# One decoder layer in float32: the output projection as three fp32r passes with weights streamed from DRAM, cross products and a bias at other steps, zeroing at other steps

## What is computed

```
x = x + attn(layernorm(x))      # 16 heads of 128, rope, causal softmax, out = sum_heads z @ W_O + b_O
x = x + xattn(layernorm(x))     # kv products of 8 x 8 channels, causal convolution with k, skip, product with ctx
x = x + moe(layernorm(x))       # 16 experts, top 4, and a shared expert
```

## Time and profile before

| | |
|---|---|
| median of 3 runs | 970.07 us (969.96 to 970.83) |
| the profiled execution | 968.15 us |
| its span, first to last instruction | 966.3 us |
| PE / DVE busy | 97% / 79% |
| ACT / POOL busy | 41% / 42% |
| mean granted clock of PE | 0.988 of full |
| moved by DMA | 161.22 MB, 167 GB/s mean |

### The profile page before, as it was taken

How to read it: one execution, slowest core, us unless ns; L and a number is a source line. 1 busy time by engine, 2 the same in 40 slices (tenths; PEclk the granted TensorE clock), 3 DMA queues, 4 the chain that set the end, 5 groups by cost and what they waited for, 6 DMA issues and landing times.

```text
span 966.3 us, 18710 instructions
## 1 busy us (share of the span) xinstructions
PE 935.6 (97%) x6081; PEld 830.0 (86%) x6081; DVE 761.1 (79%) x1692; ACT 392.9 (41%) x1153; POOL 407.4 (42%) x320
## 2 busy tenths in 40 slices
PE   6999999999999999999999999988999999999997
PEld 6788888988888888898888888876887799999985
DVE  6878967877877888777788976677677988888867
ACT  3546444443323444233364332352245444444430
POOL 1312313154412125465213546404725267777760
PEclk9999999999999999999999999999999999999998
DMA  7963297421078932205967450225151277878769
GB/s 272 314 238 144 104 353 281 185 89 65 1 247 301 373 132 89 77 35 184 329 229 281 156 178 23 98 91 213 57 208 65 60 124 131 130 129 133 127 108 321
DMA packets 64846, 161.22 MB, mean 167 GB/s; under 512 B 6640, under 2 KB 40304, under 8 KB 63600
## 3 DMA queue, kind: packets, MB, share of 16 engines
q1 hardware_dynamic: 50304, 140.97, 41.2%
q0 software_dynamic: 14448, 19.05, 12.2%
HBM read 84.72 MB, written 75.27 MB: 166 GB/s over the span
## 4 chain that ended last, share of the span: by engine, by line
PE 89%; DVE 6%; DMA 2%; issue 1%; ACT 1%; SPq 1%; POOL 0%; DVEq 0%; POOLq 0%
PE bank L499 12%; PE bank L729 11%; PE bank L501 11%; PE bank L500 11%; PE bank L747 7%; PE bank L579 6%; PE bank L880 4%; PE bank L565 3%; PE bank L602 3%; PE bank L604 3%; PE bank L603 3%; PE bank L838 2%; PE bank L848 2%; PE bank L548 2%; PE bank L550 2%; PE bank L549 2%
## 5 line engine op out<-in xcount | busy, mean ns | idle before, releaser
L1238 POOL TENSOR_TENSOR rot<-turn 128x512 f32<-128x512 f32 x64 | 93.3, 1458 | 282.7 <-DVE rtotal L1395 216.6
L1406 DVE SCALAR_TENSOR_TENSOR turn<-bank,bqk,trig 128x1024 f32<-128x1024 f32 x128 | 162.2, 1280 | 29.0 <-PE bank L501 25.9
L1301 POOL DMA_INDIRECT sums<-ysb,token_at x79 | 123.0, 1557 | 61.9 <-DMA sums<-ysb,token_at 26.2
L1268 POOL TENSOR_TENSOR kv<-c_t,v_t 128x512 f32<-128x512 f32 x64 | 67.6, 1069 | 132.4 <-PE bank L604 68.9
L729 PE MATMUL bank<-wo,z_t 128*128 128x256 f32 x512 | 115.9, 379 | 0.8 <-ACT z_t L1087 0.8
L499 PE MATMUL bank<-xt_hi,w_hi 128*128 128x512 f32 x256 | 105.4, 412 | 1.7 <-DVE xt_lo L1370 1.7
L729 PEld LDWEIGHTS bank<-wo,z_t 128*128 128x128 f32 x512 | 94.9, 190 | 12.7 <-ACT z_t L1087 1.0
L1079 ACT COPY prob_t<-bank 128x512 f32<-128x512 f32 x64 | 37.5, 586 | 164.5 <-PE bank L565 164.5
L501 PE MATMUL bank<-xt_hi,w_lo 128*128 128x512 f32 x256 | 100.1, 391 | 0.0
L1045 ACT ACTIVATE prob<-prob,negmax 128x128 f32<-128x128 f32 x256 | 99.0, 390 | 2.5 <-DVE negmax L1391 2.4
L1056 ACT COPY v<-bank 128x512 f32<-128x512 f32 x64 | 37.6, 587 | 153.4 <-PE bank L501 153.4
(11 more groups left out here) (191 smaller groups left out, 2328.5 us busy)
## 6 DMA issues: line engine op xcount, KB each, us to landing
xs<-zeros SPq DMA_DIRECT2D x16, 2120.0 KB, 13.6
w_hi<-w_dram SPq DMA_DIRECT2D x24, 768.0 KB, 4.3
w_lo<-w_dram SPq DMA_DIRECT2D x24, 768.0 KB, 7.3
xe_all<-xs SPq DMA_DIRECT2D x79, 132.5 KB
sums<-zeros SPq DMA_DIRECT2D x3, 2176.0 KB, 18.2
raw<-in_wqkv SPq DMA_DIRECT2D x16, 384.0 KB, 4.4
w_dram<-w_hi SPq DMA_DIRECT2D x8, 768.0 KB, 6.6
w_dram<-w_lo SPq DMA_DIRECT2D x8, 768.0 KB, 8.2
```

The source lines that it names most:

```text
L1238: nc.gpsimd.tensor_tensor(rot[m][1][:], turn[m][1], turn[m][2], ALU.add).then_inc(rot_pool, 1)
L1268: nc.gpsimd.tensor_tensor(kv[f % 4][:], c_t[:, :, ch].unsqueeze(3).to_broadcast(wide), v_t[:, :, ch].unsqueeze(2).to_broadcast(wide), ALU. ...
L1301: nc.gpsimd.indirect_dma_start(sums_dram[s % SUMS], bass.IndirectOffsetOnAxis(ap=token_at[:, s:s + 1], axis=0), ysb[s % YBUFS][:], None, c ...
L1406: last = nc.vector.scalar_tensor_tensor(turn_all[m][:, 2 * i:2 * i + 2, :], qk_bank[2 * m + i][:].unsqueeze(1).to_broadcast([128, 2, GT]), ...
```

## The change

- The output projection becomes a split product: 24 fp32r matmuls in a step in place of 8 plain ones. ACT now writes z with its bias into `prob_t` (free by then) and then casts it to `z_hi`; POOL makes `z_lo` (`z_low`, first in its list of each step); PE waits for both.
- `wo` becomes `wo_hi` and `wo_lo` in the same ring as the other weights. Group 0 splits them (`out_hi` on ACT, `out_lo` on DVE, two in step (0,1), one in each of (0,2) to (0,6)) and SP stores them (`keep_wo`); SP loads two more pieces, 256 KB each, with each pair's weights (`load_wo`), and a place now also waits for `wo_done`.
- POOL: `cross_kv` moves from p = 2 to 5 to p = 3 to 6, ahead of `cross_skip`; the bias `bo` from p = 5 to p = 1.
- SP: the zeroing goes by the table FILL_STEPS, whose (g,p) is the place in the loop of weight loads, which runs up to two steps ahead of the step that uses them: one or two transfers at each place of group 1, one at (2,3), one at each of (3,0) to (3,3). After the loop `gus` is loaded first, and `c_t` waits for the scatters of group 1.

```diff
+FILL_STEPS = ([(1, p) for p in range(4)] + [(1, p) for p in (4, 4, 5, 5, 6, 6, 7)] + [(2, 3)]
+              + [(GROUPS - 1, p) for p in range(4)])
...
@@ sync
+            def load_wo(q):
+                at = W_AT[q]
+                sp.dma_start(wo_hi[:, at].bitcast(F32), wo_dram[q, 0]).then_inc(w_loaded[at], 16)
+                sp.dma_start(wo_lo[:, at].bitcast(F32), wo_dram[q, 1]).then_inc(w_loaded[at], 16)
...
+                if p == 2:
+                    keep_wo(0)
+                if p > 1:
+                    keep_wo(p - 1)
...
                     sp.wait_ge(v_ready, 2 * (PAIRS * (g - 1) + W_BEFORE[p] + 1))
+                    sp.wait_ge(wo_done, PAIRS * (g - 1) + W_BEFORE[p] - 1)
...
+                    load_wo(p)
-                    if g < GROUPS - 1 and p < PARTS:
-                        fill(g - 1, p)
-                    if g == GROUPS - 1:
-                        fill(g - 1 + p // PARTS, p % PARTS)
+                    for n, at_step in enumerate(FILL_STEPS):
+                        if at_step == (g, p):
+                            fill(n // PARTS, n % PARTS)
...
@@ tensor
-                    pe.wait_ge(zt_taken, s * 2 - 4)
+                    pe.wait_ge(z_hi_done, s * 2 - 4)
+                    pe.wait_ge(z_lo_done, s * 2 - 4)
...
+                    if g == GROUPS and p > 0:
+                        pe.wait_ge(w_loaded[at], 64 * (GROUPS - 1) * W_USES[at] + 32)
                     for b in range(GB):
+                        o = acc[b // 2][:, (b % 2) * D:(b % 2 + 1) * D]
                         for h in range(2):
-                            last = nc.tensor.matmul(
-                                acc[b // 2][:, (b % 2) * D:(b % 2 + 1) * D], z_t[h][:, b, :],
-                                wo[:, 2 * r + h, :], start=(r == 0 and b % 2 == 0 and h == 0),
-                                stop=(r == PAIRS - 1 and h == 1), skip_group_check=True)
+                            nc.tensor.matmul(o, z_hi[h][:, b, :], wo_hi[:, at, h, :],
+                                             start=(r == 0 and b % 2 == 0 and h == 0), stop=False, skip_group_check=True)
+                            nc.tensor.matmul(o, z_hi[h][:, b, :], wo_lo[:, at, h, :],
+                                             start=False, stop=False, skip_group_check=True)
+                            last = nc.tensor.matmul(o, z_lo[h][:, b, :], wo_hi[:, at, h, :], start=False,
+                                                    stop=(r == PAIRS - 1 and h == 1), skip_group_check=True)
...
@@ scalar
-                            nc.scalar.activation(z_t[h][:], zt_bank[:].rearrange("p (b n) -> p b n", b=GB),
+                            nc.scalar.activation(prob_t[h][:], zt_bank[:].rearrange("p (b n) -> p b n", b=GB),
                                                  ACT.Identity, bias=bv[:, n:n + 1]).then_inc(zt_taken, 1)
...
+                        if i >= 2:
+                            act.wait_ge(zt_taken, s * 2 - 4 + h + 1)
+                            if live(3):
+                                act.wait_ge(wo_done, s - 2)
+                            nc.scalar.copy(z_hi[h][:], prob_t[h][:]).then_inc(z_hi_done, 1)
...
@@ gpsimd
+            def z_low(g, p, live):
+                s = g * PAIRS + p
+                for h in range(2):
+                    pool.wait_ge(z_hi_done, s * 2 - 4 + h + 1)
+                    nc.gpsimd.tensor_tensor(z_lo[h][:], prob_t[h][:], z_hi[h][:].bitcast(F32),
+                                            ALU.subtract).then_inc(z_lo_done, 1)
...
-                if p == 5 and live(0):
+                if p == 1 and live(0):
...
-                if g > 0 and live(0) and 2 <= p < PAIRS - 2:
+                if g > 0 and live(0) and 3 <= p < PAIRS - 1:
+                    for f in range(4):
+                        cross_kv(g - 1, 4 * (p - 3) + f)
                     if p == 3:
                         cross_skip(g - 1)
-                    for f in range(4):
-                        cross_kv(g - 1, 4 * (p - 2) + f)
...
@@ vector
+            def out_lo(q):
+                dve.wait_ge(wo_hi_done, q + 1)
+                r = wo_pair(q)
+                nc.vector.tensor_tensor(wo_lo[:, W_AT[q]], wo_raw[:, 2 * r:2 * r + 2, :],
+                                        wo_hi[:, W_AT[q]].bitcast(F32), ALU.subtract).then_inc(wo_lo_done, 1)
```

More of the change, by code:

```diff
@@ L58, with wo_pair @@
 PARTS_DOWN = EXPERTS // GB
+FILL_STEPS = ([(1, p) for p in range(4)] + [(1, p) for p in (4, 4, 5, 5, 6, 6, 7)] + [(2, 3)]
+              + [(GROUPS - 1, p) for p in range(4)])
+def wo_pair(q):
+    return (q - 2) % PAIRS
 def shared_bank(k, i):
@@ L156, in decoder @@
         prob_t = [sb(f"prob_t{h}", [128, GB, SEQ], c=tctx) for h in range(2)]
-        z_t = [sb(f"z_t{h}", [128, GB, SEQ], c=tctx) for h in range(2)]
-        wo = sb("wo", [128, HEADS, D], c=tctx)
+        z_hi = [sb(f"z_hi{h}", [128, GB, SEQ], F32R, tctx) for h in range(2)]
+        z_lo = [sb(f"z_lo{h}", [128, GB, SEQ], F32R, tctx) for h in range(2)]
+        wo_hi = sb("wo_hi", [128, WRING, 2, D], F32R, tctx)
+        wo_lo = sb("wo_lo", [128, WRING, 2, D], F32R, tctx)
         bqk = sb("bqk", [128, PAIRS, 4], c=tctx)
@@ L174, in decoder @@
         acc = banks[6:8]
+        wctx = ExitStack()
+        sb("before_wo", [128, (CROSS_AT + 4 * GB * D) // 4], c=wctx)
+        wo_raw = sb("wo_raw", [128, HEADS, D], c=wctx)
+        wctx.close()
         xctx = ExitStack()
@@ L241, in decoder @@
         wo_loaded = sem("wo_loaded")
+        wo_hi_done = sem("wo_hi_done")
+        wo_lo_done = sem("wo_lo_done")
+        z_hi_done = sem("z_hi_done")
+        z_lo_done = sem("z_lo_done")
         raw_loaded = [sem(f"raw_loaded{i}") for i in range(2)]
@@ L398, in _ @@
                 if p == 1:
-                    sp.dma_start(wo[:], wo_in).then_inc(wo_loaded, 16)
+                    sp.dma_start(wo_raw[:], wo_in).then_inc(wo_loaded, 16)
                 if p == 2:
@@ L418, in _ @@
             keep(PAIRS - 1)
+            keep_wo(PAIRS - 1)
             for g in range(1, GROUPS):
@@ L720, in step @@
                     r = (p - 3) % PAIRS
-                    pe.wait_ge(zt_taken, s * 2 - 4)
-                    if r == 0:
-                        if first:
-                            pe.wait_ge(wo_loaded, 16)
-                        else:
-                            pe.wait_ge(acc_taken, g * 2)
+                    at = W_AT[(p - 1) % PAIRS]
+                    pe.wait_ge(z_hi_done, s * 2 - 4)
+                    pe.wait_ge(z_lo_done, s * 2 - 4)
+                    if first:
+                        pe.wait_ge(wo_hi_done, p)
+                        pe.wait_ge(wo_lo_done, p)
+                    elif r == 0:
+                        pe.wait_ge(acc_taken, g * 2)
+                    if g == GROUPS and p > 0:
+                        pe.wait_ge(w_loaded[at], 64 * (GROUPS - 1) * W_USES[at] + 32)
                     for b in range(GB):
+                        o = acc[b // 2][:, (b % 2) * D:(b % 2 + 1) * D]
                         for h in range(2):
-                            last = nc.tensor.matmul(
-                                acc[b // 2][:, (b % 2) * D:(b % 2 + 1) * D], z_t[h][:, b, :],
-                                wo[:, 2 * r + h, :], start=(r == 0 and b % 2 == 0 and h == 0),
-                                stop=(r == PAIRS - 1 and h == 1), skip_group_check=True)
+                            nc.tensor.matmul(o, z_hi[h][:, b, :], wo_hi[:, at, h, :],
[4 more added lines that the diff above has]
+                                                    stop=(r == PAIRS - 1 and h == 1), skip_group_check=True)
                     last.then_inc(wo_done, 1)
@@ L992, in split_hi, with out_hi @@
                 if p >= WRING and n % CH == 0:
-                    act.wait_ge(w_stored[W_AT[p]], 32 * W_NTH[p])
+                    act.wait_ge(w_stored[W_AT[p]], 64 * W_NTH[p])
                     act.wait_ge(v_ready, 2 * (p - WRING) + 2)
                 nc.scalar.copy(w_hi[:, W_AT[p], n % CH, :], raw[n % 2][:]).then_inc(w_hi_done, 1)
+            def out_hi(q):
+                if q == 0:
+                    act.wait_ge(wo_loaded, 16)
+                if q >= WRING:
+                    act.wait_ge(w_stored[W_AT[q]], 64 * W_NTH[q])
+                if q > WRING + 1:
+                    act.wait_ge(wo_done, q - WRING - 1)
+                r = wo_pair(q)
+                nc.scalar.copy(wo_hi[:, W_AT[q]], wo_raw[:, 2 * r:2 * r + 2, :]).then_inc(wo_hi_done, 1)
             def route_exp(g):
@@ L1100, in step @@
                     split_hi(2 * p + 3)
+                    for q in range(0 if p == 1 else p + 1, p + 2):
+                        if p:
+                            out_hi(q)
                 if p == 3 and g > 1 and live(0):
@@ L1427, in step @@
                     split_lo(2 * p + 3)
+                    for q in range(0 if p == 1 else p + 1, p + 2):
+                        if p:
+                            out_lo(q)
                 if p == 0 and g > 1 and live(0):
```

25 lines of the change are left out of this document (19 added, 6 removed).

## The result

| | before | changed kernel |
|---|---|---|
| median of 14 runs each | 969.25 us (966.64 to 971.01) | 962.50 us (960.96 to 967.03) |
| the profiled execution | 968.15 us | 965.64 us |
| its span | 966.3 us | 963.8 us |
| PE / DVE busy | 97% / 79% | 96% / 81% |
| ACT / POOL busy | 41% / 42% | 45% / 52% |

The ratio is 0.9946, with a 95% interval of 0.9934 to 0.9958: faster by 0.5%, 5 to 7 us, where 13.2 were forecast.

The account below looks back on a forecast made before the run. PE, busy 97% of the span, was taken as the bound. Steps -17.4, last steps +2.3, (0,4) +0.8, (0,1) +0.6 and raw weights +0.5 gave -13.2 us: 956.9 us from 970.1, range 950 to 966.

Parts of the forecast that it names:

- the projection: Output projection's 24 split matmuls at 0.12 us each: 2.87 in place of 3.45 us, gaining 0.58 us a step, -17.4 over 30.
- passes alone: Rival: projection time follows passes through the array only, saving 0.86 us a step, -25.8, to 948.5 us; chance 0.03.
- stationary loads: Rival: the projection's 24 loads at 190 ns do not overlap, adding 1.1 us a step, about 1,005 us; chance 0.03.
- rival 5: No change to be measured: gain and new waits cancel; a measurement can tell 2 us; chance 0.04.
- POOL's order: POOL's reordered `z_lo`, `rot`, cross products and scatters meet PE's needs, tight for the first product at 416; cost 0.
- the prediction's own signs of being wrong: PE waiting for `z_lo`, cross products or weights mid-groups 1 to 3; spacing 0.14 or more; PE behind line 1422's slowed counterpart.
- the clock at 0: PE's lowered clock from 640 to 660 us, costing 1.8 us before, taken as unchanged: 0, bounds -1.8 and +3.5.
- Group 0: Extra weight splits, bias and raw weights: +0.8 us at (0,4), +0.6 at (0,1), +0.5 for raw weights.
- ACT's cast at no cost: ACT's added cast starts its exponentials 0.6 us later, but DVE asks for the sums later: cost 0 in the common step.
- The last steps: After attention's last values no projections hide z: cast and `z_lo` delay PE, +2.3 us for two steps, own gain counted.
- The first: Rival: steps with a full DVE do not shorten with PE, half of the 17.4 stays, 965 us or so; chance 0.12.
- The fourth, POOL late: Rival: POOL's list passes 21 us in 12 cross-product steps, so `z_lo` and first product hold PE, some 990; chance 0.05.

Follow-up runs that it names:

- `skip_step7`: Changed kernel with POOL's skip addition moved from p = 3 to p = 7: 983.75 us, ratio 1.0066 to before; the unedited change was not run on that chip.
- `early_order`: Changed kernel with POOL's four cross products right behind `z_lo`, and the skip behind it at p = 7: 969.81 us, ratio 0.9908, 11.5 below the unedited changed kernel.
- the fourth set's control: The changed kernel, unedited, run again on a chip without late starts: 962.91 us against 967.19 for before, ratio 0.9948.
- `early_last`: `early_order` with `z_lo` of (4,0) on DVE, its halves around the additions into x: 959.21 us, ratio 0.9902 to before.
- `combined_filler`: `combined` with 37 matmuls computing nothing wanted, placed in PE's three waits of the last steps: 961.10 us, 6.1 below `combined`, ratio 0.9855 to before.
- `bias_step5`: Changed kernel with POOL's bias addition back at p = 5: 980.10 us, 3.9 above the unedited changed kernel, ratio 1.0055 to before.
- `combined`: `early_last` with the bias addition of group 0 at p = 5, other groups' at p = 1: 967.22 us against 975.96 for before, ratio 0.9923.
- `split_alone`: Changed kernel with all the moves undone, keeping split projection, `z_lo` on POOL and streamed weights: 987.62 us, ratio 1.0101 to before.
- `scatter_next_step`: Changed kernel with each four scatters issued one step later, behind that step's `z_lo`: 983.51 us, ratio 1.0168 to before.
- `moves_alone`: Kernel before with the change's POOL order, zeroing table, bias place and end of SP's list, without the split projection: 990.20 us against 977.34, ratio 1.0152.
- the first three sets and the last: Four of five groups of follow-up runs, each sharing its runs of before; the third and last share a chip. Unedited change: second 1.0015, third 1.0037.
- the second set: Follow-up runs of the unedited change (976.21 us against 975.15, ratio 1.0015), before, and edits with the bias or the zeroing put back.
- the first set: Four follow-up kernels on one chip, without the unedited change: moves without split, split without moves, skip at p = 7, later landing wait; ratios 1.0006 to 1.0152.

## Why the prediction was right or wrong

**Right: the projection.** 0.12 us a matmul, 0.59 us a step where 0.58 stood, in every step that nothing else holds. The rivals of passes alone and of stationary loads fell. The sign and the range held; the size did not: -13.2 forecast, -5.2 by the ratio, -6.8 by the medians, near the worst end of the bounds. That the sign held is in part luck of the chip: on two later ones the same kernel gained nothing (1.0015 and 1.0037), gain and new waits cancelling as rival 5 has it.

**Wrong: POOL's order at nothing.** This step failed. The prediction says "That is tight but holds", and its sum has the order among "the rest 0"; in the pair it cost 2.5 + 1.8 = 4.3 us, the largest single error. It checked when PE needs POOL's results and found room, and room there was for the products: PE waits for none. It did not ask what stands beside the moved work, though the blocking rule was in hand, nor what `z_lo` stands behind. `skip_step7` and `early_order` show the first (2.5 us, gone). The second, scatters still landing when `z_lo` is due, was named in the text ("scatters end some 6 us later, just before the next z") and given no price; it cost 1.8 us in the pair and about the same in the fourth set's control. PE's 0.35 us for `z_lo` at (3,1) is also one of the prediction's own signs of being wrong. In `early_last`, on the chip of that control and with the scatters earlier, (3,2) is clean, -0.06 in place of +1.63; the wait alone was not isolated.

**Wrong: the clock at 0.** PE's gaps in the last steps grew from 4.0 to 7.5 us together, the longest to 3.34 at (4,1), and the clock fell in and behind them. PE in the changed kernel:

```profile
620.00:630.00 10.00, 6.54 (x33) 0.66 0.40 136
630.00:640.00 10.00, 5.94 (x37) 0.83 0.01 2
```

PE stood at the lower level for 20.5 us between 600 and 760 us in place of 10.2. That cost +4.6, less a dip of 1.5 that before has at 346 us: net +3.1, inside the bound of +3.5 but far from the 0 that was taken. `combined_filler` shows that the gaps cause the fall in the last steps: filled, the clock stays at 1.00 there. It is not the only cause of low clock: before's dips at 346 and 510 us come while PE has no wait at all, and stay unexplained.

**Group 0**, 3.2 for 1.9 in the pair, was right but for one thing: (0,3) and (0,6) together are 1.6 to 1.9 us in all four traces of the unedited change, and the 1.6 at (0,4), POOL's stretched `rot`, is in the pair's alone. `bias_step5` and `combined` point to the bias as the main cause at (0,3). **ACT's cast at no cost** was wrong in (2,2) and (3,2), 0.5 us each: the exponentials behind it were asked for earlier than I read. **The last steps** were right by their own mechanism, +1.7 for +1.7 in the terms of the budget. Two terms were not in the prediction, the 1.3 us near 904 us and the stretched `rot`. POOL's order 4.3, the clock 3.1, group 0 1.3, 904 us 1.3 and the cast 1.0 make 11.0 us, the clean steps give 0.3 back; the pair lies 10.7 above the forecast. The medians lie 6.4 above it, and traces can't share that out. One reading was wrong without effect: of the two waits of the earlier trace rows one is at 143 us, in the attention, and not in the last steps.

**Rivals.** The first had nearly the right time (965) and the wrong cause: full steps of DVE did give the gain, but for two. The fourth, POOL late, is what `split_alone` and `scatter_next_step` are; the change's own moves keep it off. That the products' move gains nothing by itself was too mild: on a chip with late starts `moves_alone` loses 1.5%; on the other kind it was not run.

**Open.** In the first three sets and the last, on three chips, traces show late starts: DVE and ACT 0.9 to 1.1 us late beside scatters in the attention, or the long wait near 750 us. The change meets the first in five or six steps where before meets it in two, some 5 to 6 us; with the longer wait near 750 us, 5.2 to 5.7 against 4.0 in before's one trace, that is most of what turns 0.995 into 1.0015 and 1.0037. That late starts fall beside scatters is what the traces of these sets show, and early_order's order does away with them in the attention; that the scatters and not the products' place matter was not separated, and why chips differ stays open. It may not be the chip alone: in the second set and the last, before's own runs fall into some of 969 to 971 us and most of 973 to 979, and no trace of one of the short ones was taken.

## What to carry to other kernels

When work moves to "idle" time of an engine, look at what runs beside it there, not only at who needs its result: a small instruction of DVE can last until the POOL instruction beside it has ended, and the other way round. Put new work that a bound engine waits for ahead of anything with a long tail, such as scatters and their landing. Price gaps of PE at their length and at the clock that they cost behind them; where a gap can't go, filling it may pay. Run the unedited kernel again in every set: the first set, without it, could not be read.

## What was not expected of the hardware

- A `rot` of POOL that takes 5.19 us beside DVE in three traces and 1.68 in the others, in the same place of the same order.
- Late starts beside scatters on some chips: 0.03 us after PE's end on one kind, 0.87 to 1.1 us on the other, up to 2.4 us in before's step (2,7). Near 750 us, where POOL issues scatters one after another, a wait of PE is 0.69 us on one kind and 4.0 to 5.7 on the other.
- Empty matmuls that save 6.1 us by keeping the granted clock at 1.00.
- The same edit is worth 0.5% in two sets and nothing in two others, on other chips: a ratio from one chip is not the ratio.
